# The product and the scan of each block of 768 columns in two instructions each, divided at the PSUM bank border and interleaved with those of the next block

## What is computed

```python
def step(h, inp):
    d_t, u_t, B_t, C_t = inp
    h = h * jnp.exp(d_t[..., None] * A) + (d_t * u_t)[..., None] * B_t[:, :, None, :]
    return (h, jnp.einsum('bkdn,bkn->bkd', h, C_t))
_, ys = jax.lax.scan(step, h0, seq)
```

## Time and profile before

| | before |
|---|---|
| runs, us | 32604.29, 32618.05, 32617.53; median 32617.53 |
| the profiled execution, us | 32605.19, span 32603.4 |
| DVE busy | 28731.8 us, 88% of the span |
| POOL busy | 22314.8 us, 68% |
| ACT busy | 15872.9 us, 49% |
| PE busy (matmul; modelled) | 24387.7 us, 75% |
| granted TensorE clock, mean | 0.909 |

### The profile page before, as it was taken

The page is one execution under the profiler, slowest core; times in us unless marked ns, Lnnn a source line. Parts: engine busy times, 40 slices in busy tenths (PEclk is TensorE's granted clock), DMA queues, the critical chain, the costliest instruction groups (busy, mean ns, idle before and its releaser), DMA issues.

```text
span 32603.4 us, 317462 instructions
## 1 busy us (share of the span) xinstructions
PE 24387.7 (75%) x78148; PEld 12020.4 (37%) x78148; DVE 28731.8 (88%) x21480; ACT 15872.9 (49%) x22789; POOL 22314.8 (68%) x12356
## 2 busy tenths in 40 slices
PE   7777777777777777777777777777777777777777
PEld 3333333333333333333333333333333333333333
DVE  8888998899888998889988898888898888988888
ACT  5444454445444454444544454444454444544444
POOL 7666766667666776667766676666676666766666
PEclk9888988899888998889889998899999889989999
DMA  4333433334333333334333343333343333433333
GB/s 133 105 106 104 133 114 106 105 110 137 106 106 104 120 127 105 106 105 133 114 103 112 109 140 118 112 112 113 121 135 112 112 112 109 139 118 112 112 113 121
DMA packets 1409449, 3759.43 MB, mean 115 GB/s; under 512 B 204384, under 2 KB 204512, under 8 KB 1404896
## 3 DMA queue, kind: packets, MB, share of 16 engines
q1 hardware_dynamic: 1407328, 3736.27, 35.2%
HBM read 3659.95 MB, written 47.19 MB: 114 GB/s over the span
## 4 chain that ended last, share of the span: by engine, by line
issue 47%; DVE 36%; PE 13%; ACT 2%; POOL 2%; DVEq 1%; DMA 0%; SPq 0%; POOLq 0%; ACTq 0%
DVE ps L1153 23%; DVE arena L487 5%; DVE arena L1157 4%; PE ps L673 3%; PE ps L577 1%; PE ps L827 1%; PE ps L826 1%; PE ps L661 1%; PE ps L645 1%; PE ps L622 1%; POOL arena L1295 1%; DVEq L1155 1%; PE ps L814 0%; PE ps L815 0%; DVE arena L484 0%
## 5 line engine op out<-in xcount | busy, mean ns | idle before, releaser
L1295 POOL TENSOR_TENSOR arena<-arena 128x768 f32<-128x768 f32 x9216 | 16682.3, 1813 | 5310.9 <-DVE arena L1157 4937.5
L673 PE MATMUL ps<-arena,consts 128*128 128x384 f32 x36864 | 14075.2, 506 | 369.4 <-ACT arena L1007 190.5
L1157 DVE TENSOR_TENSOR_SCAN arena<-arena,carry,ps 128x768 f32<-128x768 f32 x6144 | 11143.7, 1814 | 672.7 <-DVE ps L1153 33.8
L954 ACT ACTIVATE arena<-arena,An 128x768 f32<-128x768 f32 x9216 | 8578.1, 934 | 4428.8 <-POOL arena L1295 3674.3
L661 PE MATMUL ps<-arena,consts_b 96*128 96x512 bf16 (+1 forms) x18432 | 4751.7, 341 | 6201.4 <-DVE arena L1157 5993.0
L1153 DVE TENSOR_TENSOR ps<-ps,arena 128x768 f32<-128x768 f32 x9216 | 8681.6, 942 | 251.1 <-PE ps L661 246.5
L673 PEld LDWEIGHTS ps<-arena,consts 128*128 128x128 f32 x36864 | 6477.1, 196 | 4750.1 <-issue 571.7
L1157 DVE TENSOR_TENSOR_SCAN arena<-arena,ps 128x768 f32<-128x768 f32 x3072 | 5387.3, 1754 | 348.7 <-ACT arena L954 30.7
L661 PEld LDWEIGHTS ps<-arena,consts_b 96*128 96x128 bf16 x18432 | 1312.6, 100 | 11433.8 <-DVE arena L1157 10183.1
L984 ACT COPY carry<-arena 128x1 f32<-128x1 f32 x6144 | 1166.6, 190 | 6130.9 <-DVE arena L1157 6129.8
L487 DVE SCALAR_TENSOR_TENSOR arena<-arena,wp 128x2304 f32<-128x2304 f32 (+1 forms) x896 | 2332.3, 2603 | 31.6
(11 more groups left out here) (157 smaller groups left out, 18671.1 us busy)
## 6 DMA issues: line engine op xcount, KB each, us to landing
arena<-c_rows SPq DMA_DIRECT2D x6144, 384.0 KB, 3.5
arena<-c_rows SPq DMA_DIRECT2D x6144, 192.0 KB, 3.3
arena<-arena SPq DMA_DIRECT2D x384, 72.0 KB, 2.0
c_rows<-arena SPq DMA_DIRECT2D x32, 576.0 KB, 4.5
arena<-x SPq DMA_DIRECT2D x17, 864.0 KB, 4.3
arena<-mid SPq DMA_DIRECT2D x17, 864.0 KB, 4.4
mid<-arena SPq DMA_DIRECT2D x16, 864.0 KB, 4.7
out<-arena SPq DMA_DIRECT2D x16, 864.0 KB, 4.1
```

Of the source, the lines that this page charges most:

```text
L673: mm = pe.matmul(y_part[:, h, :], ident, hC[it % NW][:, h * SEG:(h + 1) * SEG], start=(n == 0), stop=(n == NS - 1))
L954: act.activation(state_at[it % NW], delta[g % 2], ACT.Exp, scale=An[:, slot(s) * NS + n:slot(s) * NS + n + 1]).then_inc(sem["da_ready"], 1)
L1157: dve.tensor_tensor_scan(a[:, ::back], a[:, ::back], slots[it % 2][:, ::back], 0.0 if k == 0 else carry[:, n:n + 1], ALU.mult, ALU.add).th ...
L1295: pool.tensor_tensor(hC[it % NW], state_at[it % NW], Csb[b], ALU.mult).then_inc(sem["hc_ready"], 1)
```

## The change

DVE's product and scan are each made of two instructions, one of 512 and one of 256 columns, divided where the slot passes from one PSUM bank to the next. Forward groups take the 512 first, backward groups the 256. Between the parts stand those of the next block: first part of scan i, first part of product i + 1, second part of scan i, second part of product i + 1. The first part of the scan starts from 0 or from `carry`, as the whole one did; the second part always starts from the last column of the first, read through a pointer from `state_at`. Two semaphores are new, `dbu_first` and `scanned_first`. `dbu_ready` and `scanned`, for which the other engines wait, are raised by the second parts. The gate of layer 0 (`gate_sums`) moves from behind the work of n = 4 to behind that of n = 3, since product 5 would else wait for PE's broadcast 5, which stands behind an `add_state` that waits for this gate. The programs of PE, ACT, POOL and SP stay as they are.

```diff
@@ the semaphores
-    "b_bcast": NIT, "da_ready": NIT, "dbu_ready": NIT, "scanned": NIT, "hc_ready": NIT, "y_summed": NIT,
+    "b_bcast": NIT, "da_ready": NIT, "dbu_first": NIT, "dbu_ready": NIT, "scanned_first": NIT, "scanned": NIT, "hc_ready": NIT, "y_summed": NIT,
@@ DVE
-            def scan(g):
-                s, p, j, k, c = group(g)
-                back = -1 if p else 1
-                for n in range(NS):
-                    it = NS * g + n
+            def parts(p):
+                return [slice(0, BANK), slice(BANK, CH)][::-1 if p else 1]
+
+            def input_part(it, q):
+                g, n = it // NS, it % NS
+                o = parts(group(g)[1])[q]
+                if q == 0:
                     if n == 0:
                         dve.wait_ge(sem["du_ready"], v("du_ready", g + 1))
                     dve.wait_ge(sem["b_bcast"], v("b_bcast", it + 1))
-                    dve.tensor_tensor(slots[it % 2], slots[it % 2], du[g % 2], ALU.mult).then_inc(sem["dbu_ready"], 1)
+                done = sem["dbu_first"] if q == 0 else sem["dbu_ready"]
+                dve.tensor_tensor(slots[it % 2][:, o], slots[it % 2][:, o], du[g % 2][:, o], ALU.mult).then_inc(done, 1)
+
+            def scan_part(it, q):
+                g, n = it // NS, it % NS
+                s, p, j, k, c = group(g)
+                back = -1 if p else 1
+                o = parts(p)[q]
+                a = state_at[it % NW]
+                if q == 0:
                     dve.wait_ge(sem["da_ready"], v("da_ready", it + 1))
+                    dve.wait_ge(sem["dbu_first"], v("dbu_first", it + 1))
+                    first = 0.0 if k == 0 else carry[:, n:n + 1]
+                    done = sem["scanned_first"]
+                else:
                     dve.wait_ge(sem["dbu_ready"], v("dbu_ready", it + 1))
-                    a = state_at[it % NW]
-                    dve.tensor_tensor_scan(a[:, ::back], a[:, ::back], slots[it % 2][:, ::back],
-                                           0.0 if k == 0 else carry[:, n:n + 1], ALU.mult, ALU.add).then_inc(sem["scanned"], 1)
-                    if At.layer == 0 and n == 4 and g > NG - NC:
+                    dve.wait_ge(sem["scanned_first"], v("scanned_first", it + 1))
+                    first = a[:, BANK:BANK + 1] if p else a[:, BANK - 1:BANK]
+                    done = sem["scanned"]
+                dve.tensor_tensor_scan(a[:, o][:, ::back], a[:, o][:, ::back], slots[it % 2][:, o][:, ::back],
+                                       first, ALU.mult, ALU.add).then_inc(done, 1)
+
+            def scan(g):
+                for n in range(NS):
+                    it = NS * g + n
+                    if it == 0:
+                        input_part(0, 0)
+                        input_part(0, 1)
+                    scan_part(it, 0)
+                    if it + 1 < NIT:
+                        input_part(it + 1, 0)
+                    scan_part(it, 1)
+                    if it + 1 < NIT:
+                        input_part(it + 1, 1)
+                    if At.layer == 0 and n == 3 and g > NG - NC:
                         gate_sums(g - 1)
```

## The result

| | before | after |
|---|---|---|
| median, us | 32617.79 (four runs, 32604.29 to 32635.45) | 33289.47 (four runs, 33269.81 to 33318.42) |
| ratio to before | | 1.0206, 95% interval 1.0189 to 1.0224 |
| the profiled execution, us | 32605.19, span 32603.4 | 33318.42, span 33316.6 |
| DVE busy, instructions | 28731.8 us, 21480 | 29483.4 us, 39912 |
| granted TensorE clock, mean | 0.909 | 0.916 |

The changed kernel is 672 us slower, inside the range and 380 us short of the forecast. Between the two spans it is 713. The scan phases of the 32 passes, from the first product to the last scan, grew by 704 us (25793 to 26498); the other phases together by 9. Those other phases have the same program in all kernels here and take 6788 to 6833 us in their traces, so that a difference of some 40 us between two kernels need not come from the scan.

The account below looks back on a forecast made before the run. DVE alone was taken to set the pace, without slack. The terms 46 + 393 + 139 + 245 + 80 + 186 - 21 gave +1068 us on 32605.2, so 33673, stated as 33670 us; range 33150 to 34150.

Parts of the forecast that it names:

- body: DVE's own time with four instructions a block: 2.780 us with a carry, .005 more than before, +46 us.
- block 4 and the rest of 5: Broadcast late behind the matmuls of the next group's delta, at 313 of 544 places, and the next product: +393 us.
- block 10: Three groups, 96 places behind the merge of u: DVE waits longer for PE's broadcast, +139 us.
- block 13: Backward directions, 288 places behind four extra matmuls at n = 8: the broadcast, hidden before, comes late, +245 us.
- block 15: Last backward groups, 96 places: the broadcast, released later through the stall at block 13, comes late, +80 us.
- border: Between groups the first product, now earlier, waits for GpSimd's du: +186 us.
- gate: Layer 0's gate, 32 places, moved before scan 4, whose first part (.66 us) now stands inside its wait: -21 us.
- Rival (b): Pointer reads of DVE's scans hide in the full queue, -922 us: +146 in all, 32.75 ms; chance .07.
- The broadcast is asked for earlier: Next block's first product precedes the second scan: release to need 1.44 us forward, 1.17 backward, before some 2.7.
- rival (a): Half clock at block 4 goes because PE's rhythm differs, 391 us fall away: +677, 33.28 ms; chance .14.
- (c): Queued DVE instructions' starts hide down to the product's .059, no pointer cost: block 2.664, -75 us, 32.53 ms; chance .04.
- (d): No overlap behind a product, a scan cannot start before its end: +1530 us more, 35.20 ms; chance .06.

Follow-up runs that it names:

- pe_spread: Changed kernel with PE's extra matmuls (those of n = 8, n = 10 and the merge) placed one to a state: 32700.63 us, 1.0029.
- no_pointer: Changed kernel with the second part of each scan started from the constant 0 instead of the first part's last column: 32854.23 us, 1.0074.
- split_only: Changed kernel in the order product, product, scan, scan of one block, nothing of the next block between, gate at its old place: 34173.35 us, 1.0478.
- pool_early: Changed kernel with GpSimd's four steps for the next group's delta one block earlier each: 33075.55 us, 1.0142.
- spread_early: all_moved with the two delta matmuls together again at n = 3, that is pe_spread and pool_early in one kernel: 32567.45 us, 0.9987.
- all_moved: Changed kernel with PE's extra matmuls spread, delta's two matmuls at n = 2 and 3, and GpSimd's steps one block earlier: 32242.84 us, 0.9885.
- all_parts: all_moved with the broadcast's two matmuls released and handed on one by one: 32332.21 us, 0.9918.
- whole_moved: Kernel before, undivided, with the same three moves of PE's and GpSimd's work as all_moved: 32529.38 us, 0.9974.
- halves: Changed kernel divided at column 384 instead of the bank border 512, so one part crosses the border: 33190.91 us, 1.0177.

## Why the prediction was right, and where it was off

The direction, the mechanism of the waits and their places held; one term, DVE's own time, was mis-sized, and two erred by less. That the waits add up to 1269 where 1268 were forecast is luck: blocks 4 and 5 came out 95 below their forecast and the other four places 93 above it in sum, and the wait at block 4 alone goes from 207 us (pe_spread) to 310 (no_pointer) between kernels whose edits were not made for it. All in us, between the spans:

| step | forecast | measured |
|---|---|---|
| body | +46 | -338 |
| block 4 and the rest of 5 | +393 | 302 + 39 - 42 = +299 |
| block 10 | +139 | 231 - 83 = +148 |
| block 13 | +245 | +271 |
| block 15 | +80 | +90 |
| border | +186 | +234 |
| gate | -21 | 32 x 3.09 - 121 = -22 |
| sum | +1068 | +682, of +713 |

31 us are in no row of this; 9 of them lie outside the scan phases.

- **The body is the term that was mis-sized.** The step was ".059 of its own per product" and for the scan ".071 of its own without a pointer and .131 with one". Measured are .049 (.582 - .533), .060 (1.127 - 1.067) and .121 (.654 - .533), .010 less for each of four instructions. I had taken the scan's cost from scans that had waited for their product, and put on a product the overlap of .08 that stands behind a scan. Neither is the case in a full queue. A scan of 256 columns that waited lasts .746 (split_only), one behind a busy instruction .736; of 512 it is 1.280 and 1.270. And a product overlaps its follower by .09 (.673 long, .582 to the next start). The earlier trace rows had the hint: L1175 is .85 from start to start, .05 above its data, and the text rounded it away by taking the other figure. Four times .010 in each of 9216 blocks is 370 us, nearly all of the 384 between +46 and -338; the text had allowed for .02 a block, 184 us. Its size, not the mechanism: the gain of interleaving is there (split_only: 1945 us) and pays for two more instructions, where the text said "Nothing is won there": 338 us are won.
- **"I take the pointer as paid"** held, .12 with two of them in a block (no_pointer: -.060 for one). Rival (b) is out.
- **"The broadcast is asked for earlier"** held as the cause of the loss. From the end of the scan to the need there are .316 + 1.187 - .084 = 1.42 forward (forecast 1.44) and .582 + .654 - .084 = 1.15 backward (1.17). Blocks 10, 13 and 15 came out 4 to 13% above the forecast, and pe_spread removes all three.
- **Block 4** had nearly the right price and the wrong number of places. The forecast's 313 are those at which adding the state lasted over 1.7 us in the trace before, 167 of them forward. In the trace after these are 202, 56 of them forward, and they cost 282 us; at the forecast's prices, 1.12 forward and 1.39 backward, they would cost 266. Most of the other 20 us (15) is at 32 places that the forecast left out: in the first group of a pass no state is added there yet, but PE is at half clock, and the broadcast is .48 late. So rival (a), the half clock gone at block 4, came true in part, at about a third of the 313 places. I had kept it apart as a case of all or nothing with .14, where the number of places itself moves with the program.
- **The border** is 48 us more than the forecast. Its waits number 400 on the timeline, .50 each (200.8 us of idle time); pool_early shows that nothing but POOL's du is behind it.
- **The gate** held: 3.09 each where 3.80 - .66 = 3.14 was forecast.
- **Rivals (c) and (d).** A block is 2.739, .075 above the 2.664 that decided for (c): the pointers and the scans' own start did not hide. (d) is out: products overlap the scans behind them by .09. The Trainium skill (VectorE: DVE Perf Modes, The DRAIN you can't avoid) says that a following operation starts only when the pipe is empty, and adds that one which is not held starts earlier; the prediction took the first half alone. In these rows an independent follower starts .08 to .09 us before the end, a dependent one .10 behind it. The Trainium skill (Vector Engine (DVE) Microarchitecture Reference, 5.2 Measured stream behaviour on trn2) gives about 75 ns for each instruction after queue overlap. It lies between the 49, 60 and 121 ns measured here. The estimate of 2.700 for each block by it was .039 off the 2.739 and .021 off the 2.679, mine .041 both times; over the run it is 553 us under mine (.080 in 6144 blocks, .020 in 3072), and not the 513 of the text, so a total of +515.

**Left open** is why the half clock comes at block 4 in one program and not in another. pe_spread and spread_early have the same PE program and differ in the states at which POOL does its four steps; the one has 109 long places, the other 288. The runs of one kernel go with it too: pe_spread's lie from 32664 to 32754 us, the shorter at a mean granted clock of 0.920, the longer at 0.916. What the runs show is where it is met. The trace after has 5.6 ms of half clock, 4.0 of them outside the scan phases and .5 in the first group of each pass, where it has lasted since before. The other 1.1 ms is in blocks n = 1 to 6 of PE's row. 388 of the 9216 additions of a state last over 2 us, all of them at half clock: 194 at n = 3, right behind the delta's matmuls of 12 rows, 158 at the next state, n = 4, 36 at n = 1, 2 and 5, and none at the others. Placing the delta's matmuls one to a state does not remove the half clock, but it makes these places fewer and moves them: from spread_early to all_moved, which differ in that alone, the long additions fall from 458 to 174 and those at n = 3 from 288 to 30, while 67 appear at n = 2. That is not the same in each program either: with the same placing, all_parts has 139, 71 and 88 of them at n = 2, 3 and 4, and whole_moved 131, 84 and 76.

## What to carry to other kernels

Dividing dependent instructions and interleaving them with those of the next block removes the wait between them, but it also puts the next block's first read in front of the rest of this block's work. Before such a change, list for every producer the time between release and need, after the change, and the places where the producer is behind by more; then place that producer's additional work one by one. Here the moves alone gained 0.26%, dividing and interleaving alone lost 2.06%, and both together gained 1.15%. Cost an instruction by the distance of starts in a full queue and not by its duration less an overlap seen elsewhere: .010 us on each of four instructions a block was 370 us, about the error of 380.

## What the runs showed of the hardware

- A scan behind a busy instruction lasts .010 us less than one that had waited (.736 and .746 for 256 columns), a product .027 (.406 and .433). A product right behind another product lasts .421 (split_only). A product on PSUM overlaps its follower by .09, a scan by .08. A dependent follower instead starts .10 to .11 behind the end (463.98 against 462.60 + 1.27 in split_only). Together .18 to .20 for each such pair.
- The scan's start from a pointer costs .06 us, whether the queue is full or not.
- An instruction that crosses from one PSUM bank to the next costs nothing more: .542 and 1.004 us on either side in halves.
- The half clock behind small matmuls does not follow from PE's own program alone: there are 109 places with POOL's steps late (pe_spread) and 288 with them one state earlier (spread_early). It is no rule of these steps either: the same move between after and pool_early leaves 194 and 198.
